# Separate staging buffers for queries and keys, and a ring of four slots of two heads instead of three of four

## What is computed

```python
x = _layernorm(x + _L0_attn_ref(x, ...), axis=-1)            # Gaussian "splat" attention, 16 heads of 16
x = _layernorm(x + _L0_xattn_ref(x, ctx_512, ...), axis=-1)  # cross attention, 16 heads of 16, 120 keys
x = _layernorm(x + _L0_ffn_ref(x, ...), axis=-1)             # best of 8 experts
x = _layernorm(x + _L1_attn_ref(x, ...), axis=-1)            # causal attention, 16 heads of 16
x = _layernorm(x + _L1_xattn_ref(x, ctx_512, ...), axis=-1)  # self, then cross attention, 16 heads of 32
x = _layernorm(x + _L1_ffn_ref(x, ...), axis=-1)             # best 4 of 16 experts
```

## Time and profile before

| what | value |
|---|---|
| median of 3 runs | 4110.17 us (4107.24, 4110.17, 4129.73) |
| the profiled execution | 4104.28 us |
| its span, first to last instruction | 4102.6 us |
| TensorE busy | 3208.5 us, 78% |
| VectorE busy | 2695.7 us, 66% |
| ScalarE busy | 2103.1 us, 51% |
| GpSimd busy | 975.7 us, 24% |
| mean granted TensorE clock | 0.884 |

### The profile page before, as it was taken

How to read it: one execution, slowest core, us unless ns; L and a number is a source line. 1 busy time by engine, 2 the same in 40 slices (tenths; PEclk the granted TensorE clock), 3 DMA queues, 4 the chain that set the end, 5 groups by cost and what they waited for, 6 DMA issues and landing times. The chain is left out here.

```text
span 4102.6 us, 87404 instructions
## 1 busy us (share of the span) xinstructions
PE 3208.5 (78%) x34864; PEld 2496.1 (61%) x34864; DVE 2695.7 (66%) x6135; ACT 2103.1 (51%) x4254; POOL 975.7 (24%) x1793
## 2 busy tenths in 40 slices
PE   2878687888687878877977868797867797878776
PEld 1666465766575657656755657575646675756654
DVE  5767575766575757756766657585756676757665
ACT  4645464555455555544554545545545555446542
POOL 1312341122122321221233122211332122114310
PEclk9989898988898989888988989898988897989987
DMA  6221211112112111121111111212111112112110
GB/s 185 73 59 49 70 53 55 48 51 65 45 53 68 48 58 54 39 65 52 56 57 58 51 51 40 66 52 63 60 50 52 50 44 71 50 54 67 53 36 6
DMA packets 339974, 233.26 MB, mean 57 GB/s; under 512 B 67937, under 2 KB 311538, under 8 KB 339570
## 3 DMA queue, kind: packets, MB, share of 16 engines
q1 hardware_dynamic: 339570, 227.68, 18.8%
HBM read 122.23 MB, written 105.38 MB: 55 GB/s over the span
## 5 line engine op out<-in xcount | busy, mean ns | idle before, releaser
L1164 ACT ACTIVATE p<-bank,p_log 128x512 f32<-128x512 f32 (+2 forms) x1280 | 749.6, 586 | 1118.3 <-PE bank L855 1013.6
L1718 POOL TENSOR_TENSOR prob<-p,prob 120x256 f16<-120x256 f32 (+2 forms) x512 | 452.3, 883 | 1841.4 <-ACT prob L1165 1841.0
L1423 DVE TENSOR_REDUCE negm<-bank 128x2 f16<-128x512 f32 (+1 forms) x1280 | 675.4, 569 | 147.6 <-PE bank L818 140.1
L1165 ACT ACTIVATE prob<-bank,p_log 128x512 f16<-128x512 f32 (+2 forms) x1280 | 751.2, 587 | 0.0
L834 PE MATMUL bank<-q_ring,k_ring 80*128 80x256 f16 (+4 forms) x2048 | 459.2, 292 | 124.6 <-DVE made L1374 90.7
L1353 DVE TENSOR_TENSOR prob<-p,prob 128x512 f16<-128x512 f32 (+2 forms) x768 | 481.3, 636 | 94.0 <-ACT prob L1165 90.3
L725 PE MATMUL bank<-w_exp,ident_h 128*128 128x512 f16 x1280 | 426.3, 418 | 133.9 <-DMA k_ring<-k_heads 121.2
L855 PE MATMUL bank<-ident_h,negm 128*128 128x256 f16 (+2 forms) x2560 | 456.6, 267 | 0.0
L818 PE MATMUL bank<-k_ring,q_ring 80*128 80x256 f16 (+4 forms) x2560 | 373.7, 262 | 75.9 <-DVE negm L1423 62.8
L818 PEld LDWEIGHTS bank<-k_ring,q_ring 80*128 80x128 f16 (+1 forms) x2560 | 239.0, 105 | 283.8 <-DVE negm L1423 72.4
L1727 POOL TENSOR_SCALAR_AFFINE_SELECT probm<-prob 128x128 f16<-128x128 f16 x1024 | 323.8, 354 | 342.5 <-DVE prob L1353 342.5
(11 more groups left out here) (295 smaller groups left out, 6307.0 us busy)
## 6 DMA issues: line engine op xcount, KB each, us to landing
q_ring<-q_heads SPq DMA_DIRECT2D x192, 160.0 KB, 2.6
q_heads<-made SPq DMA_DIRECT2D x192, 128.0 KB
k_heads<-made SPq DMA_DIRECT2D x192, 128.0 KB
q_heads<-made SPq DMA_DIRECT2D x96, 256.0 KB
k_heads<-made SPq DMA_DIRECT2D x96, 256.0 KB
q_ring<-q_heads SPq DMA_DIRECT2D x128, 192.0 KB, 2.7
k_ring<-k_heads SPq DMA_DIRECT2D x128, 160.0 KB, 2.8
k_ring<-k_heads SPq DMA_DIRECT2D x64, 192.0 KB, 3.1
```

Source lines behind the costliest of these rows:

```text
L1164: act(p32[0:n, g % PBUF32, 0:cols], ps[0:n, 0:cols], ACT.Exp, bias=p_log[0:n, :], scale=a.scale)
L1165: act(prob[0:n, 0, g % PBUF, 0:cols], ps[0:n, 0:cols], ACT.Exp, bias=p_log[0:n, :], scale=a.scale).then_inc(a_done, one(a_done))
L1423: v.tensor_reduce(negm[:, h * NT:(h + 1) * NT], ring_v[bank_of(e, v_full)][:, :].rearrange("p (t n) -> p t n", t=NT)[:, :, 0:ATTNS[k].keys ...
L1718: g.tensor_tensor(prob[0:n, 1, m % PBUF, 0:cols], p32[0:n, m % PBUF32, 0:cols], prob[0:n, 0, m % PBUF, 0:cols], ALU.subtract).then_inc(pp_ ...
```

## The change

There are two staging buffers, one for queries and one for keys; each waits only for the store of its own content of the phase before. Heads of 16 store three planes too (high, low, high for queries; high, high, low for keys; the product of the two low parts is dropped), and the plane that is left out is filled with zeros once, so that the stacked height of 80 rows stays. The ring has four slots of two heads; a fill is placed three pairs ahead of its use, waits for the exact scores of the pair four before, and moves half as much. In `LATE_SOON` for `k` = 3 "xT", "q" and "k" move from turns 23, 25, 27 to 22, 24, 25.

```diff
-QUAD, QUADS, SLOTS = 4, 4, 3
-Q_PLANES = (0, 1, 0, 1)
-K_PLANES = {3: (0, 0, 1), 4: (0, 0, 1, 1)}
+SLOTS = 4
+PLANES = {"q": (0, 1, 0), "k": (0, 0, 1)}
...
-LATE_SOON = {..., 3: (("xT", 23), ("q", 25), ("k", 27), ("v", 28))}
+LATE_SOON = {..., 3: (("xT", 22), ("q", 24), ("k", 25), ("v", 28))}
...
 def stored_ahead(k, b, what):
-    if what == "k":
-        return STORED[k, b, "q"]
     p = PHASE[k, b]
-    return STORED[(*PHASES[p - 1], "k")] if p > 0 else 0
+    return STORED[(*PHASES[p - 1], what)] if p > 0 else 0
...
-        made = pair("made", 4, TOK)
-        q_ring, k_ring = (sb(f"{what}_ring", [96, SLOTS, QUAD, TOK], F16) for what in "qk")
+        made = {what: pair(f"{what}_made", 4, TOK) for what in "qk"}
+        q_ring, k_ring = (sb(f"{what}_ring", [96, SLOTS, PAIR, TOK], F16) for what in "qk")
...
-                        if g % QUAD == 0:
-                            e.wait_ge(ring_full[g // QUAD % SLOTS], slot_filled(g // QUAD))
+                        if g == pair[0]:
+                            e.wait_ge(ring_full[g // PAIR % SLOTS], slot_filled(g // PAIR))
...
-                        if g % QUAD == QUAD - 1:
-                            freed["ring", g // QUAD] = a_full, sent(a_full)
+                    freed["ring", pair[0] // PAIR] = a_full, sent(a_full)
...
-                def fill(quad):
+                def fill(m):
...
-                    if quad >= SLOTS:
-                        e.wait_ge(*moved("ring", quad - SLOTS))
+                    if m >= SLOTS:
+                        e.wait_ge(*moved("ring", m - SLOTS))
...
-                        e.dma_start(ring[0:a.stacked, quad % SLOTS, :, 0:cols],
-                                    heads_dram(what, k, b)[c:c + QUAD, :, t, 0:cols].rearrange("c r n -> r c n")
-                                    ).then_inc(ring_full[quad % SLOTS], 16)
+                        e.dma_start(ring[0:a.stacked, m % SLOTS, :, 0:cols],
+                                    heads_dram(what, k, b)[c:c + PAIR, :, t, 0:cols].rearrange("c r n -> r c n")
+                                    ).then_inc(ring_full[m % SLOTS], 16)
...
-                        begin = max((2 * quad - 4) * TURNS + 2, PLACE[(k, b), "k"] + 0.5)
+                        begin = max((m - SLOTS + 1) * TURNS + 2, PLACE[(k, b), "k"] + 0.5)
```

More of the change, by code:

```diff
@@ L169 @@
 }
-LATE_SOON = {1: (("xT", 18), ("q", 21), ("k", 23), ("v", 28)), 3: (("xT", 23), ("q", 25), ("k", 27), ("v", 28))}
+LATE_SOON = {1: (("xT", 18), ("q", 21), ("k", 23), ("v", 28)), 3: (("xT", 22), ("q", 24), ("k", 25), ("v", 28))}
 VECTOR_ONLY = ("out2", "experts3", "norm4", "h3", "r3", "ctx2")
@@ L1275, in between_attentions @@
                             if a.causal:
-                                raw_tiles(a.tiles, n, made, bias)
+                                raw_tiles(a.tiles, n, made[what], bias)
                             else:
                                 for m in range(0, a.tiles, 2):
-                                    highs((made[:, 0, m:m + 2, 0:n], lambda ps: two(ps)[:, :, 0:n], 1 / W_SCALE))
+                                    highs((made[what][:, 0, m:m + 2, 0:n], lambda ps: two(ps)[:, :, 0:n], 1 / W_SCALE))
                             yield
@@ L1387, in split_heads @@
                     n = a.keys if what == "k" else TOK
+                    high, low = (made[what][:, part, 0:a.tiles, 0:n] for part in range(2))
                     if not a.splat and not a.causal:
                         for m in range(0, a.tiles, 2):
-                            lows(made[:, 1, m:m + 2, 0:n], made[:, 0, m:m + 2, 0:n],
+                            lows(low[:, m:m + 2, :], high[:, m:m + 2, :],
                                  lambda ps: ps[:, :].rearrange("p (t n) -> p t n", t=2)[:, :, 0:n], 1 / W_SCALE)
                         return
-                    at = next_half(what, k, b)
-                    tiles = raw[:, at:at + a.tiles, 0:n]
+                    r = next_half(what, k, b)
+                    tiles = raw[:, r:r + a.tiles, 0:n]
                     if a.causal:
-                        last = low_part(made[:, 1, 0:a.tiles, 0:n], tiles, made[:, 0, 0:a.tiles, 0:n])
+                        last = low_part(low, tiles, high)
                     else:
@@ L1400, in split_heads @@
                         if what == "q":
-                            last = split(tiles, made[:, 0, 0:a.tiles, :], made[:, 1, 0:a.tiles, :])
+                            last = split(tiles, high, low)
                         else:
                             for t in range(KT):
-                                last = split(raw[:, at + t, 0:n], made[:, 0, t, 0:n], made[:, 1, t, 0:n],
-                                             k_scale[:, t:t + 1])
+                                last = split(tiles[:, t, :], high[:, t, :], low[:, t, :], k_scale[:, t:t + 1])
                     last.then_inc(split_done, one(split_done))
```

35 lines of the change are left out of this document (17 added, 18 removed).

## The result

The changed kernel takes 3825.18 us (median of 4 runs, 3815.62 to 3827.75), the kernel before, on the same chip, 4110.07 us: ratio 0.9293 (95% interval 0.926 to 0.9326), 285 us less. The forecast was 3815. On another chip the same kernel took 3816.13 us, ratio 0.9283 (0.9264 to 0.9301).

A forecast was written before the change was run, and what follows sets the result against it. TensorE's idle time was taken as the bound, chiefly staging waits behind the queries' store and ring waits. Terms -143 - 10 - 40 - 24 - 3 - 96 + 12 + 12 = -292 from 4104.3 gave 3812, forecast 3815 us; range 3740 to 3890.

The forecast's parts named there:

- The staging wait: TensorE waiting for staged tiles' low parts, apart from close phases of k = 3: the wait goes, -143 us.
- The close k = 3 phases: Six phases where queries' store, keys' store and first fill follow each other unhidden: 27.9 us becomes 22.4, -40 us in all.
- The 1.2 us for a turn earlier: In the six close phases of k = 3, everything starting a turn earlier was counted as worth 1.2 us each.
- Ring waits in total: Sign to look for: TensorE's waits for ring fills over the whole span stay near 120 us.
- The close k = 1 phases: Six phases with waits for row maxima and ring: keys' store begins earlier with three DMAs, 4 us each, -24 us.
- the ring: 640 pairs filled by 1280 DMAs instead of 640: the lead just holds and hides them, cost 0.
- the planes: Heads of 16: zeros for 16 more rows and the planes left out cost nothing on the path.
- The clock: Low granted clock behind 32 of 46 staging waits, 3.1 us each, is won back: -96 us, bounds nothing and -150.
- Fills behind stores: Fills of pairs 6 and 7 now queue behind both stores: 4 us in three short phases, +12 us.
- Rival A: Store bandwidth bounds more than six phases, keys stored 26 us after the queries' store begins: +144, 3960 us; chance 0.20.
- Rival B: Slower through the ring's shorter lead, deciding from about 9 us a fill: 4200 us; chance 0.06.
- on a queue that mostly waits. Cost 0 if it holds: SyncE's issues for the added ring fills, 0.3 to 0.5 us each, were taken to cost 0.

The follow-up runs named there:

- wide store: Changed kernel, each store of heads of 32 sent as eight transfers with 32 outermost on the DRAM side, instead of three DMAs: 3738.88 us, ratio 0.9092.
- the same, fills first: Three slots and wide store, with fills of pairs 0 to 6 placed 2.7 turns earlier on SyncE, ahead of stores and context loads: 3760.3 us, ratio 0.9137.

## Why the prediction was right, and where it wasn't

**The staging wait** was read rightly: 221.5 us of TensorE's waits became 24.3. The other terms of idle time sum to -196 in the prediction (-143 - 10 - 40 - 24 - 3 + 12 + 12); measured are -203.

**The sum** is nearer than its terms, and in part by luck. One buffer against two gives the second buffer 153 us of idle time, where its terms are 143 + 10 + 40 and a part of the 24; the rest of the change gives 49.5 us of idle time (894.1 to 844.6), where I had put it at about nothing. One was too high and the other too low, and the two misses cancel.

**The close k = 3 phases.** The queries' store to the release of the fill was put at 19.2 us and is 19.0 to 19.5. The wait for the fill was to end 22.4 us behind the queries' store and ends 21.5 to 22.0 behind it in all six, since a fill lands in 2.5 us and not in 3.2. The waits left, put at about 12, are 13.0 to 14.8, since TensorE comes to them 7.2 to 8.7 us behind the store and not 10.0. The 1.2 us for a turn earlier were a mistake: with the old places nothing is lost. What the chain depends on is the first store and the transfer time of both. Ring waits in total were to stay near 120 us and are 143.6: these six, and the 23 us inside phases.

**The close k = 1 phases and the rest.** The wait for the bias fell by 28 us, where I had 24 for these phases; their ring waits rose from 26.7 to 30.2. But the sum had hidden a shift between terms: with one buffer the rest of the change already gains 44.5 us, where I gave the ring, the planes and the places next to nothing (-3 and +12, and a part of the 24). The planes are 18 of it. If these add up, 26 are left, in which the places have no share (0 us by their own run). In the one-buffer run the ring waits at the starts of phases are 88.8 us where the kernel before has 121.2, and 12.5 come inside phases. The smaller first fill is a likely part of this, not separated here: fills of 80 KB land in 1.9 to 2.1 us, and I had gone by 2.5 to 2.8.

**The clock.** Put at -96 us, by the count of 32 waits times 3.1 us, which is 99. Busy time fell by 86.5, and by 96.6 between one buffer and two. That the ring's waits were left out of the count was right by its result only: I had no reason for it, and expected 4 to 5 us a wait when I came to test it. They didn't go away in the changed kernel (19 waits before, 24 after). Over the runs busy time goes with how many ring waits there are, and not with how long they are:

| kernel | ring waits | their length, us | TensorE busy, us |
|---|---|---|---|
| changed | 24 | 143.6 | 3122.0 |
| wide store | 17 | 68.5 | 3126.4 |
| three slots | 110 | 315.6 | 3201.2 |
| three slots, wide store | 95 | 177.4 | 3180.7 |
| the same, fills first | 40 | 83.7 | 3140.0 |

Against the changed kernel that is 0.8 to 1.1 us of busy time for each added wait. No run takes the waits away and leaves all else as it is, so that the count is the cause is the reading that fits and not shown by itself.

**Fills behind stores.** +12 us in three short phases; the waits inside phases are 23 us, 16.3 of them in three phases. The mechanism was right. Rival A's price for it (144 us) needed a keys' store at 26 us behind the queries', and it stayed at 19.

**Rival B**, the shorter lead, got 0.06 and didn't come. But it was nearer than its chance says. I had priced it by a fill's landing time alone, deciding from 9 us on, and the three-slot run, where the median from issue to landing is 3.3 us or less at every place of a phase, lost 195 us. The step of the prediction that fails is "on a queue that mostly waits. Cost 0 if it holds": SyncE's list is worked off in order, and while it waits for one item's data it holds back the fills behind it, 128 of the 133 us inside phases in the run with three slots and the wide store. With four slots the margin covered it; nothing in my working had shown that.

## What to carry to other kernels

When a buffer is waited for because its store is slow, look first at how many DMA engines that store runs on: spreading it gave nearly as much here as a second buffer, and both together more than either. A ring's lead has to be counted from the release of the slot to the need, through everything that stands ahead of the fill on its issuing queue, and an item whose data is late belongs behind the fills, not ahead of them. In this kernel shortening a wait gave back its length alone, and waits that went away gave back the low clock behind them too (the second buffer: 153 us of idle time and 97 of busy time): behind waits of 3 to 6 us the next 7 us ran as low (0.65) as behind those of 13 to 15 us (0.71).

## What the runs showed of the hardware that was not expected

- For heads of 32 (three DMAs of 256 KB on four engines) the keys' store took longer to issue when it came close behind the queries': 3.85 to 4.14 us at 4.2 us behind it, 4.81 to 5.65 at 2.9 to 3.4 us, against 1.68 to 1.70 in the kernel before, at 12 us and more. Stores of three DMAs of 128 KB (heads of 16) didn't: 1.80 to 1.83 us in after even at less than 4 us behind the other.
- More and smaller transfers were the faster store: eight of 64 to 128 KB at 208 GB/s against three of 256 KB at 88 to 99 GB/s, with a DMA share of 0.93 against 0.25.
- The first 7 us behind a wait of TensorE ran at a granted clock of 0.60 in the mean for waits of 5 to 8 us, 0.65 for 3 to 6 us and 0.71 for 13 to 15 us: the length of the wait hardly matters for what follows it.
